# Two layers of expert FFN on one core: four dense tiles instead of two, two token groups instead of three, and a pipeline one step deeper

## The reference, cut to what matters

```
x = x + block1(layernorm(x), token_ids, ctx)    # ctx: 4 experts, each a 256x256 matrix W, used three times
    e = min(clip(id, 0, 12499) // 3125, 3)
    y = (silu(h @ W[e].T) * (h @ W[e].T)) @ W[e].T       # gate, up and down are the same W
x = x + block2(layernorm(x), Wg, W1, W2, W3)    # 8 experts of hidden width 176, all computed densely
    two best scores of h @ Wg.T, softmax over the two -> w[token, expert]
    y = sum_e w[:, e] * ((silu(h @ W1[e].T) * (h @ W2[e].T)) @ W3[e].T)
```

## Time and profile before

| | us |
|---|---|
| median of three runs | 172.8 |
| profiled execution | 172.57 |
| its span | 170.7 |
| TensorE busy | 148.3 (87% of the span) |
| VectorE busy | 104.5 (61%) |
| ScalarE busy | 67.3 (39%) |
| GpSimd busy | 42.8 (25%) |
| rests of block 2's weights on GpSimd (L332, 11 of them) | 20.1 |

### The profile page before, as it was taken

The page is one execution under the profiler, slowest core; times in us unless marked ns, Lnnn a source line. Parts: engine busy times, 40 slices in busy tenths (PEclk is TensorE's granted clock), DMA queues, the critical chain, the costliest instruction groups (busy, mean ns, idle before and its releaser), DMA issues.

```text
span 170.7 us, 2812 instructions
## 1 busy us (share of the span) xinstructions
PE 148.3 (87%) x999; PEld 137.5 (81%) x999; DVE 104.5 (61%) x280; ACT 67.3 (39%) x143; POOL 42.8 (25%) x43
## 2 busy tenths in 40 slices
PE   5935999866797999467999999899999999999991
PEld 1323867756796999367989999799999999999990
DVE  2687466697459688983463589564545457455352
ACT  3262156765795683125133242722232232232230
POOL 0104567946446189284000002000000000000000
PEclk9999699999999999955899999999999999999999
DMA  4999412200446512003000001000000002000002
GB/s 85 288 410 398 116 40 67 60 0 0 132 108 216 162 52 78 0 0 92 6 0 0 0 4 61 0 0 4 0 0 2 0 6 92 0 0 4 0 0 92
DMA packets 5710, 10.98 MB, mean 64 GB/s; under 512 B 993, under 2 KB 2657, under 8 KB 5697
## 3 DMA queue, kind: packets, MB, share of 16 engines
q1 hardware_dynamic: 4832, 8.84, 15.8%
q0 software_dynamic: 720, 1.97, 4.4%
q10 hardware_dynamic: 144, 0.00, 0.0%
HBM read 8.58 MB, written 2.23 MB: 63 GB/s over the span
## 4 chain that ended last, share of the span: by engine, by line
PE 56%; DVE 18%; ACT 9%; issue 8%; DMA 5%; POOL 1%; DVEq 0%; SPq 0%; POOLq 0%; ACTq 0%
PE bank L877 26%; PE bank L893 16%; PE bank L778 3%; PE bank L780 3%; PE bank L779 3%; DMA raw<-y_rows,slot 3%; DMA x_sb<-x_dram 3%; ACT h L388 2%; DVE act L740 2%; ACT norm L415 2%; DVE stats L617 2%; DVE act L592 2%; DVE act L597 1%; ACT silu L475 1%; PE bank L836 1%
## 5 line engine op out<-in xcount | busy, mean ns | idle before, releaser
L877 PE MATMUL bank<-hT_hi,w_hi 128*128 128x384 f32 (+1 forms) x132 | 43.2, 328 | 2.4 <-DVE gated L735 2.4
L877 PE MATMUL bank<-hT_hi,w_lo 128*128 128x384 f32 (+1 forms) x132 | 42.9, 325 | 0.0
L877 PE MATMUL bank<-hT_lo,w_hi 128*128 128x384 f32 (+1 forms) x132 | 42.9, 325 | 0.0
L484 ACT ACTIVATE silu<-bank 128x384 f32<-128x384 f32 (+1 forms) x33 | 15.0, 455 | 58.5 <-PE bank L877 58.5
L735 DVE TENSOR_TENSOR gated<-gate,bank 128x384 f32<-128x384 f32 (+1 forms) x33 | 16.8, 508 | 28.8 <-PE bank L877 27.9
L675 DVE TENSOR_TENSOR act_lo<-act,act_hi 128x384 fp32r<-128x384 f32 (+1 forms) x33 | 22.5, 682 | 11.7 <-ACT act_hi L438 10.9
L877 PEld LDWEIGHTS bank<-hT_hi,w_hi 128*128 128x128 f32 x132 | 25.8, 195 | 2.6 <-issue 2.6
L893 PE MATMUL bank<-w_hi,act_lo 128*128 128x256 f32 x88 | 25.9, 294 | 0.6 <-DVE act_lo L675 0.6
L877 PEld LDWEIGHTS bank<-hT_hi,w_lo 128*128 128x128 f32 x132 | 25.8, 196 | 0.0
L877 PEld LDWEIGHTS bank<-hT_lo,w_hi 128*128 128x128 f32 x132 | 25.7, 195 | 0.0
L893 PE MATMUL bank<-w_lo,act_hi 128*128 128x256 f32 x88 | 25.1, 285 | 0.0
(11 more groups left out here) (103 smaller groups left out, 234.4 us busy)
## 6 DMA issues: line engine op xcount, KB each, us to landing
raw<-weights_dram SPq DMA_DIRECT2D x11, 384.0 KB, 6.1
raw<-weights_dram SPq DMA_DIRECT2D x4, 256.0 KB, 5.0
y_rows<-xg SPq DMA_DIRECT2D x4, 256.0 KB, 2.2
x_sb<-x_dram SPq DMA_DIRECT2D x1, 768.0 KB, 9.1
out_dram<-x_sb SPq DMA_DIRECT2D x3, 256.0 KB, 2.3
x_sb<-x_dram SPq DMA_DIRECT2D x1, 256.0 KB, 4.3
out_dram<-x_sb SPq DMA_DIRECT2D x2, 128.0 KB, 2.3
xg<-x_dram,from_x POOLq DMA_INDIRECT x9, 3.4
```

Source lines behind the costliest of these rows:

```text
L484: nc.scalar.activation(silu[:, q % BUFFERS, 0:n], z_of(q)[0], ACT.Silu).then_inc(silu_done, 1)
L877: return nc.tensor.matmul(o, w[:, c, cols], toks[:, g % 2, k, 0:n], skip_group_check=True, **flags)
```

## The change

- `DENSE` goes from 2 to 4: 4 dense tiles (NP = 8 steps) and 4 sorted ones in N1 = 7 tiles (NS = 4 steps), so NA = 12 steps and 4*4 + 7 = 23 units. Seven fetches instead of nine, four bring-backs instead of six.
- `up1` alternates between two PSUM banks, `a_hi` and `a_lo` have two buffers (in the memory of block 2's second group), and `down1(s-2)` is issued in iteration s. `up1(s)` now stands ahead of `transpose_act(s-1)`; on ScalarE the silu ahead of `a_round`; on VectorE `act_of` ahead of `x_low` and `a_low`. The inverse permutation's fetch list (`sources`) moves into step 0.
- Block 2 has two groups of 4 tiles: `up` has 12 matmuls of 512 columns, 22 chunks in all; `up(0)` follows block 1's loop and is not inside it. x2 and its statistics are made in three parts (`SUMS`), the last one of four tiles.
- The rests of pieces 0, 2, 4, 6 and 8 are found by VectorE at the end of its iteration, one iteration after ScalarE rounds the piece; the other six by GpSimd. The ring has 5 pieces, and a load waits for the rest of the piece five before it.
- The scores take two matmuls for each tile and half (16 and 8 columns) instead of three of 8 columns; VectorE adds the two parts with two more small instructions.

```diff
-DENSE = 2
+DENSE = 4
+X_TILES = [(0,), (1,), (2, 3)] + [tuple(DENSE + t for t in tiles) for tiles in SLOT_STEPS]
+LN_TILES = [(0, 1), (2, 3)] + X_TILES[3:]
+X_AT = {0: 1, 2: 2} | {NP - 2 + k: 3 + k for k in range(NS)}
-GROUPS = ((0, 1), (2, 3, 4), (5, 6, 7))
+GROUPS = ((0, 1, 2, 3), (4, 5, 6, 7))
+SUMS = ((0, 1), (2, 3), (4, 5, 6, 7))
-RING = 7
+RING = 5
-WARM = (4, 14)
+WARM = (4, 16)
 STAGES = {
+    "sum": (("A", 6), ("A", NA - 2), ("B", 5)),
+    "shift": (("A", 7), ("A", NA - 1), ("B", 6)),
+    "normalise": (("A", 7), ("A", NA - 1), ("B", 6)),
+    "transpose_tokens": (("A", NA), ("B", 7)),       # tokens_hi and tokens_lo the same
+    "scores": (("A", NA + 1), ("B", 8)),             # best_two and tanh the same
+    "softmax": (("A", NA + 1), ("B", 9)),
+    "transpose_gates": (("B", 1), ("B", 10)),
+    "gates_out": (("B", 0), ("B", 10)),
 }
+ROUND_AT = {("A", 1 + c): (c,) for c in range(CHUNKS)}
+VECTOR_LO = (0, 2, 4, 6, 8)
...
 # GpSimd
             deviation(0)
+            deviation(1)
             pool.wait_ge(from_x_done, 1)
+            for i in range(N1):
                 fetch(i)
             deviation(2)
             deviation(3)
             weight_lo(1)
             deviation(4)
             deviation2(0)
+            weight_lo(3)
             deviation(5)
+            weight_lo(5)
+            weight_lo(7)
+            deviation2(1)
+            weight_lo(9)
+            weight_lo(10)
...
 # ScalarE
+            for s in range(NA + 2):
+                if s - 3 >= NP:
+                    take_y(s - 3 - NP)
                 if s < NA:
                     silu1[:, 0:width(s)] <- up1_bank[s % 2][:, 0:width(s)]
+                if 1 <= s <= NA:
+                    a_round(s - 1)
+                if s in X_AT:
+                    x_round(X_AT[s])
+                if s == 1:
+                    normalise(2)
+                if 4 <= s < 4 + NS:
+                    normalise(s - 1)
                 stages("A", s)
...
 # VectorE
+            def weight2_lo(c):
+                dve.wait_ge(w2_hi_done, c + 1)
+                nc.vector.tensor_tensor(w2_lo[:, c, :], raw2_piece(c), w2_hi[:, c, :].bitcast(F32),
+                                        ALU.subtract).then_inc(w2_lo_vector, 1)
...
+            for s in range(NA + 2):
+                for m in due("sum", "A", s):
+                    sum_and_statistics(m)
                 if s < NA:
                     act_of(s)
+                if s in X_AT:
+                    x_low(X_AT[s])
+                if 1 <= s <= NA:
+                    a_low(s - 1)
                 if s == 0:
+                    sources()
                     weight1_lo(2)
                     weight1_lo(3)
+                    statistics(1)
+                    shifts(1)
...
+                if 4 <= s < 4 + NS:
+                    shifts(s - 2)
+                if 3 <= s < 3 + NS:
+                    statistics(s - 1)
                 stages("A", s)          # weight2_lo(c) last, for c rounded in iteration s - 1
...
 # TensorE
+            for s in range(NA + 2):
                 if s < NA:
                     up1(s)
+                if 1 <= s <= NA:
+                    transpose_act(s - 1)
+                if s in X_AT:
+                    transpose_x(X_AT[s])
                 if s == 0:
                     pe.wait_ge(placed, 1)
...
                 stages("A", s)
+                if s >= 2:
+                    down1(s - 2)
+            for q in range(NB + LAG):
                 if q < NB:
                     up(q)
                 stages("B", q)
```

More of the change, by code:

```diff
@@ L160, in ffn_moe @@
         shift2 = sb("shift2", [P, TILES])
-        norm = sb("norm", [P, 3, D])
+        norm = sb("norm", [P, 4, D])
+        part = sb("part", [P, TILES, E2])
+        score = sb("score", [P, TILES, E2])
         top = sb("top", [P, TILES, 8])
@@ L244, in x_width, with ln_of, h1_place, span @@
         def x_width(xs):
[L245 to L252, removed]
+            return len(X_TILES[xs]) * D
+        def ln_of(xs):
+            return (0, 0, 1)[xs] if xs < 3 else xs - 1
+        def h1_place(xs):
+            return (0, 1, 2)[xs] if xs < 3 else 2 * ((xs - 3) % 2)
+        def span(tiles):
+            return slice(tiles[0], tiles[-1] + 1)
         def src_row(i):
             return x_sb[:, i, :] if i < DENSE else xg[:, i - DENSE, :]
[L257 to L261, removed]
+        def group_of_sum(m):
+            return 0 if m < 2 else 1
         def z_of(q):
-            n = tokens(group_of(q))
             pair = (4, 0)[q % 2] if group_of(q) == 0 else (0, 2)[(q - CHUNKS) % 2]
[L267 to L272, removed]
+            return bank[pair], bank[pair + 1]
+        def wait_lo(engine, c):
+            if c in VECTOR_LO:
+                engine.wait_ge(w2_lo_vector, VECTOR_LO.index(c) + 1)
+            else:
+                engine.wait_ge(w2_lo_pool, c + 1 - len([v for v in VECTOR_LO if v < c]))
         @block.sync
@@ L458, in _ @@
             x_round(0)
+            normalise(1)
             weight1_hi(2)
@@ L461, in _ @@
             act_e.wait_ge(router_in, 16)
[L462 to L470, removed]
+            nc.scalar.copy(router_hl[:, :, 0, :], router_raw[:]).then_inc(router_hi_done, 1)
+            for s in range(NA + 2):
+                if s - 3 >= NP:
+                    take_y(s - 3 - NP)
                 if s < NA:
@@ L685, in stages @@
             def stages(kind, i):
-                for g in due("shift", kind, i):
-                    shifts2(g)
-                for g in due("sum", kind, i):
-                    sum_and_statistics(g)
+                for m in due("shift", kind, i):
+                    shifts2(m)
                 for g in due("tokens_lo", kind, i):
@@ L695, in stages @@
                     softmax_gates(g)
+                for c in ROUND_AT.get((kind, i - 1), ()):
+                    if c in VECTOR_LO:
+                        weight2_lo(c)
             nc.vector.memset(warm_sb[:], 0.0).then_inc(warm_in, 1)
```

348 lines of the change are left out of this document (150 added, 198 removed).

## The result

Four runs of the changed kernel gave 175.0 to 177.77 us, median 177.07; four of the kernel before 172.59 to 174.32, median 173.55. The ratio is 1.0246, 95% interval 1.0173 to 1.032: slower by 1.7 to 3.2%. Some executions of every kernel here show a lower granted clock than others and take longer; a ratio compares only the faster ones of both kernels, while a median is over all of them. The profiled execution took 177.62 us, its span is 175.8, 5.1 us more than before.

What follows compares the result with a forecast made beforehand. Block 1 was taken as bound by waits between engines, then by a closed ScalarE-VectorE round; TensorE fills block 2. The walk's 173.4 us plus 2.1 for the clock gave 175.5 us, range 174 to 178.5.

Steps and rivals of the forecast that it cites:

- the walk: Step-by-step timing through both blocks: block 2 starts at 67.4 us, profiled time 173.4 us before the clock's price.
- The round: Block 1 from step 4: ScalarE and VectorE hand over in one closed chain of 4.0 us, setting the pace.
- step 6: Block 1: sum of tiles 0 and 1 ahead of act_of(6), x_low and a shift wait make it 5.9 us.
- step 5: Block 1: shifts(3) comes while GpSimd has weight_lo(1), adding 0.7 us to the round.
- The two waits of block 2: TensorE waits 1.5 us at up(2) for the gates and 1.9 us after up(7) for the normalises.
- those of `weight2_lo`: VectorE's weight2_lo(6) and weight2_lo(8) each wait 1.4 us on a GpSimd rest; each takes 1.0 us itself.
- The start: Before block 1's steps: up1(0) at 10.2 us, up1(1) at 15.4, low clock of 17.1 to 20.5 us kept.
- step 4: Block 1: its silu starts at 27.1 us, and from here the closed round sets the pace.
- The clock term: A clock fall near 0.5 around 62 to 70 us, priced at 2.1 us between nothing and 5.
- The port rule: VectorE and GpSimd exclude each other on SBUF, whichever starts first; without a lock both ways 0.7 us lower.
- the six added units: Block 1 has 23 units for 17; six more add 6 x 1.65 = 9.9 us of TensorE work.

Runs made afterwards that it cites:

- e12: Changed kernel with 18 idle matmuls of 512 columns on TensorE where it waits; 174.5 us, ratio 1.008 to the kernel before.
- e5: Changed kernel without the product of rounded activation and weight's rest in all block 1 matmuls; 173.5 us, ratio 1.0115 to the kernel before.
- e2: Changed kernel with VectorE's shifts at the top of an iteration, ahead of act_of, x_low and a_low; 177.8 us, ratio 1.037 to the kernel before.
- e3: Changed kernel with the sums of x2 behind act_of, x_low and a_low; executions of 176.4, 176.7, 179.4 and 179.4 us, no interval.
- e7: Changed kernel with ScalarE's rounding of pieces 3 to 10 moved out of steps 4 to 8, some rests moved too; 172.2 us, ratio 0.990.
- e6: Kernel before with VectorE finding the rests of pieces 7 to 10 in block 2; executions of 168.0, 169.9, 173.6 and 173.7 us, no interval.
- e11: Kernel before with e6's rests, six idle matmuls at 14 us and the second group's sum one chunk later; 169.3 us, ratio 0.983.
- e1: Changed kernel with all eleven weight rests on GpSimd; 175.6 us, ratio 1.023 to the kernel before.
- e4: Changed kernel with down1(s-1) instead of down1(s-2) in iteration s; 203.4 us, ratio 1.186 to the kernel before.
- e9: e7 with shifts first, GpSimd's first rest behind block 1's last deviation, gate transposes, last sum and GpSimd rests 9, 10 moved; 172.4 us, ratio 1.000.

## Why the prediction was right

**The direction and the walk.** 175.5 us was forecast, in a range of 174 to 178.5, and slower at 0.49; 177.07 was measured. The walk's parts against the trace:

| part | walk | trace |
|---|---|---|
| `up1(1)` starts | 15.4 | 16.45 |
| silu 4 | 27.1 | 30.13 |
| silu 4 to silu 8 | 19.7 | 19.96 |
| silu 8 to block 2's `up(0)` | 20.6 | 20.5 |
| block 2 starts | 67.4 | 70.57 |
| from there to its last matmul | 99.9 | 101.3 |

**The round** was right in kind, and in size at every step: 4.0, 4.7, 5.9, 5.1 forecast, 3.93, 4.40, 5.62, 5.18 in e12, where silu 3 was not late. In the changed kernel's own trace the first is 4.76: `act_of(3)` began late, and `x_low` and the statistics behind it kept `act_of(4)` until 1.46 us after its silu, for 0.63 in e12:

```profile
31.59 0.88 DVE L596 SCALAR_TENSOR_TENSOR act<-bank,mask,silu 128x256 f32<-128x256 f32 x2
...
29.24 0.88 DVE L596 SCALAR_TENSOR_TENSOR act<-bank,mask,silu 128x256 f32<-128x256 f32 x2 [0.64 <-ACT silu L467]
```

So the fit of 19.7 to 19.96 over four steps is partly luck: the walk was 0.6 us long against e12's 19.13, and the late silu gave 0.8. The terms of step 6 as written, 4.0, 1.2, 0.6 and 0.7, add up to 6.5 and not to the 5.9 taken. The trace has 0.55 for the sum (`act_of(6)` 1.17 us behind its silu, for 0.62 in step 5), 0.60 for `x_low` and 0.55 for the shift. e5 shows that TensorE's work is not in the round, as long as TensorE does not wait itself (e2, e3); the chain of ScalarE's trace and e7 show that ScalarE's is. The two waits of block 2, 1.5 and 1.9 forecast, were 1.56 and 1.46; those of `weight2_lo`, 1.4 twice, were 1.26 and 1.34, and its own price 0.95 for the 1.0 taken. Block 2 came out 9.7 us shorter, with waits of 1.56 and 1.46 us and no GpSimd rest in it; that the rests' absence made the gain is argued from the rows, and e6 and e11 test it only in part.

**The start was mis-sized** for the profiled execution, by 3.1 us, and that is the whole lateness of block 2's start. 1.05 came before `up1(1)`; the low clock lasted 6.8 us instead of the 3.4 kept from the earlier trace rows; and silu 3 started 2.0 us after its matmuls had ended (26.4), on a wait that the trace puts down to nothing in the program ("remote"). What that was stays open. From silu 2 to silu 4 it took 7.4 us here and 6.7 to 7.0 in e1, e2 and e3, which makes about half a microsecond; step 4 lost another 0.8. Much of this changes from one execution to the next: with the same list up to step 3, `up1(1)` started at 15.49 and silu 4 at 26.58 in e3, which had no low clock at the start; in e2 these were 15.63 and 28.71. The walk's 15.4 and 27.1 lie near the better of the two.

**The clock term** was right in kind: a fall from 70.3 to 73.7 us, forecast for around 62 to 70 with block 2 at 67.4. In it the 512-column matmuls started 0.43 us apart instead of 0.23, 1.4 us in all; 2.1 was taken. Over the walk's 173.4 the profiled execution has 4.2 us more: 3.2 at block 2's start and 1.4 of low clock behind it, less small change. The sum of 175.5 held because its range was wide enough for the start, not because 2.1 was the price there. In e1's trace, a kernel that differs in the rests alone, the clock did not fall near 70 us, so a fall there is not certain.

**The port rule** came out in its direction as the Trainium skill (SBUF — State Buffer, "SBUF: two separate sides") has it. The 1.34 us of GpSimd's square root beside VectorE's rest is the direction that no row of before showed: the trace agrees. With the shift held behind GpSimd's rest (0.64 us for 0.15) it made step 5 longer by 0.47 us (4.40 for 3.93), not by the 0.7 that the sum held for it. On who goes first the traces are not at one with the rule: in the earlier trace rows VectorE's `act_lo` is recorded as starting 0.14 us before GpSimd's rests and was held by them all the same.

**What was not tried:** four dense tiles alone, without the deeper pipeline or the groups of four. e4 undoes the depth on TensorE and e1 the split of the rests; no run parts the other pieces of the change. That the six added units cost 9.9 us of TensorE is worked out from rows, not shown by a run; e5 shows that most of block 1's TensorE work lies beside the round and is not paid one for one.

## What to carry to other kernels

When no engine is full (in block 1 TensorE was busy for 48.8 of 60.6 us and the others less), follow one iteration through the lists of ScalarE and VectorE: an instruction that waits for the other engine and stands ahead of the next iteration's first step closes a round, and the round, not the busiest engine, sets the pace. Take out of it what need not be there before deepening the pipeline, and compare steps between several traces: one execution can hold a delay that the others do not have. In this kernel a long GpSimd operation on SBUF belonged where VectorE worked from PSUM, and cost most where it was released by the event that releases a short VectorE operation on the path.

## What the hardware showed beside this

- Executions of the kernel before on one chip went with their mean granted clock: 170.7 to 171.0 us at 0.978, 172.4 to 172.7 at 0.96 to 0.97, 173.9 to 174.5 at 0.94 to 0.95, though two at 0.98 took 171.8 and 172.0.
- The first stretch of lower clock changed between traces with the same list up to there: none in e3, 3.4 us in e1, 6.8 us in the changed kernel and in e2.
- The kernel with 18 idle matmuls took 1.6% less although eight of them ran at the low clock themselves: in e12 these took 3.47 us at 14.3 us, 0.4 apart.
- Between a VectorE and a GpSimd operation on SBUF that were released together, the one that started 0.05 us earlier (33.64 for 33.69) held the other for its whole length, 1.8 us. A VectorE operation of 0.68 us that is recorded as starting together with two GpSimd rests (91.40 in e9) took 2.38.
